# Scores of the first query tile as three products of high and low parts

## What is computed

```python
x = L0_attn_x                                  # (4, 256, 512)
xn = _layernorm(x, axis=-1)
q = _rope((xn @ wq).reshape(B, S, 32, 128), pos)
k = _rope((xn @ wk).reshape(B, S, 8, 128), pos)
v = (xn @ wv).reshape(B, S, 8, 128)
scores = einsum('bqhgd,bshd->bhgqs', q.reshape(B, S, 8, 4, 128), k) * 128 ** -0.5
allowed = (j <= i) & (j > i - 128)             # i query, j key
attn = softmax(where(allowed, scores, finfo.min))
s = einsum('bhgqs,bshd->bqhgd', attn, v).reshape(B, S, 4096) @ wo
g = silu(ffn(xn))                              # 4-bit weights, 1376 hidden
return x + s * g
```

## Time and profile before

| | |
|---|---|
| median of 3 runs | 824.97 us |
| the profiled execution's own time | 827.23 us |
| its span, first to last instruction | 824.8 us |
| TensorE's granted clock over the span | 1.000 of full speed |
| DMA, mean over the span | 54 GB/s |

### The profile page before, as it was taken

The page is one execution under the profiler, slowest core; times in us unless marked ns, Lnnn a source line. Parts: engine busy times, 40 slices in busy tenths (PEclk is TensorE's granted clock), DMA queues, the critical chain, the costliest instruction groups (busy, mean ns, idle before and its releaser), DMA issues.

```text
span 824.8 us, 13612 instructions
## 1 busy us (share of the span) xinstructions
PE 813.2 (99%) x4024; PEld 682.1 (83%) x4024; DVE 556.8 (68%) x1640; ACT 436.3 (53%) x1141; POOL 484.5 (59%) x367
## 2 busy tenths in 40 slices
PE   7999999999999999999999999999999999999997
PEld 4888888888878888888888888888888888888886
DVE  5677757653677667584948576766758494858684
ACT  3432312213866738574666666475747465665762
POOL 1232312326666748674675667486748665677997
PEclk9999999999999999999999999999999999999999
DMA  8434322022011101200020102012001201020112
GB/s 243 131 94 149 109 64 84 29 86 77 15 38 37 41 1 52 77 2 25 25 76 0 51 13 64 0 51 67 9 0 51 76 0 51 0 76 0 52 40 102
DMA packets 43594, 44.55 MB, mean 54 GB/s; under 512 B 3492, under 2 KB 28454, under 8 KB 43558
## 3 DMA queue, kind: packets, MB, share of 16 engines
q1 hardware_dynamic: 43264, 44.05, 18.3%
q10 hardware_dynamic: 296, 0.09, 0.1%
HBM read 42.03 MB, written 2.10 MB: 54 GB/s over the span
## 4 chain that ended last, share of the span: by engine, by line
PE 93%; ACT 2%; DVE 2%; issue 1%; POOL 1%; DMA 1%; SPq 0%; DVEq 0%; POOLq 0%; ACTq 0%
PE bank L1198 26%; PE bank L1199 26%; PE bank L1200 26%; PE bank L1312 3%; PE bank L1334 3%; PE bank L1352 2%; PE bank L1353 2%; PE bank L1354 2%; PE bank L1361 1%; PE bank L1359 1%; PE bank L1358 1%; PE bank L1302 1%; PE bank L1208 1%; DVE probs L993 1%; ACT gate L638 1%
## 5 line engine op out<-in xcount | busy, mean ns | idle before, releaser
L1198 PE MATMUL bank<-xh,wih 128*128 128x512 f32 x384 | 155.2, 404 | 0.3 <-DVE k L950 0.3
L1200 PE MATMUL bank<-xh,wil 128*128 128x512 f32 x384 | 150.0, 391 | 0.0
L1199 PE MATMUL bank<-xl,wih 128*128 128x512 f32 x384 | 150.0, 391 | 0.0
L345 POOL TENSOR_TENSOR swap<-swap,cst 128x512 f32<-128x512 f32 x80 | 106.6, 1333 | 67.7 <-ACT swap L575 67.7
L608 ACT ACTIVATE probs<-probs,nmx 128x128 f32<-128x128 f32 x256 | 99.9, 391 | 71.2 <-DVE nmx L975 70.6
L1198 PE MATMUL bank<-woh,oh 128*128 128x512 f32 x256 | 100.3, 392 | 0.1
L1199 PE MATMUL bank<-wol,oh 128*128 128x512 f32 x256 | 100.0, 390 | 0.0
L1200 PE MATMUL bank<-woh,ol 128*128 128x512 f32 x256 | 99.7, 389 | 0.0
L349 POOL TENSOR_TENSOR q<-q,swap 128x512 f32<-128x512 f32 x64 | 91.3, 1427 | 8.9 <-DVE q L950 5.2
L329 POOL TENSOR_TENSOR wil<-raw,wih 128x512 fp32r<-128x512 f32 x48 | 63.5, 1359 | 42.5 <-ACT wih L557 42.5
L369 POOL TENSOR_TENSOR ph<-ph,cst 128x512 fp32r<-128x512 f32 x32 | 42.0, 1312 | 75.3 <-ACT ph L624 75.3
(11 more groups left out here) (119 smaller groups left out, 1922.0 us busy)
## 6 DMA issues: line engine op xcount, KB each, us to landing
raw<-in_wq SPq DMA_DIRECT2D x32, 256.0 KB, 2.8
raw<-in_wo SPq DMA_DIRECT2D x32, 256.0 KB, 2.9
pk<-in_w SPq DMA_DIRECT2D x44, 128.0 KB, 3.5
sc<-in_s SPq DMA_DIRECT2D x36, 128.0 KB, 3.5
pk<-in_w SPq DMA_DIRECT2D x11, 256.0 KB, 2.5
sc<-in_s SPq DMA_DIRECT2D x11, 256.0 KB, 3.2
xn<-in_x SPq DMA_DIRECT2D x8, 256.0 KB, 5.2
raw<-in_wk SPq DMA_DIRECT2D x8, 256.0 KB, 3.1
```

Source lines behind the costliest of these rows:

```text
L345: nc.gpsimd.tensor_tensor(v, v, spread(sin.unsqueeze(1), P, 2, SEQ), ALU.mult).then_inc(sin_done, 1)
L1198: nc.tensor.matmul(out_, sh, mh, start=(i == 0), stop=False)
L1199: nc.tensor.matmul(out_, sh, ml, start=False, stop=False)
L1200: m = nc.tensor.matmul(out_, sl, mh, start=False, stop=(i == n - 1))
```

## The change

The first query tile gets high and low parts too, `qh0` and `ql0`, in two new SBUF tensors. `kq_hi` and `kq_lo` issue one more instruction for each head. The plain product is replaced by `three` over 128 columns, the keys' parts as they are; `klq_done` is waited for ahead of it, and the wait for `rope_done` on TensorE is gone.

```diff
+        qh0 = sb("qh0", [P, GH, 2, P], f32r, main)
+        ql0 = sb("ql0", [P, GH, 2, P], f32r, main)
...
-        def second(ap):
-
-            return ap.rearrange("p (b t n) -> p b t n", b=2, t=2)[:, :, 1, :]
+        def tiles_of(ap, t):
+
+            return ap.rearrange("p (b t n) -> p b t n", b=2, t=2)[:, :, t, :]
...
-                    nc.scalar.activation(qh[:, c - 1], second(q[:, c - 1]), ACT.Copy).then_inc(khq_done, 1)
+                    nc.scalar.activation(qh0[:, c - 1], tiles_of(q[:, c - 1], 0), ACT.Copy)
+                    nc.scalar.activation(qh[:, c - 1], tiles_of(q[:, c - 1], 1), ACT.Copy).then_inc(khq_done, 1)
...
-                    nc.vector.tensor_tensor(ql[:, c - 1], second(q[:, c - 1]), qh[:, c - 1].bitcast(f32),
+                    nc.vector.tensor_tensor(ql0[:, c - 1], tiles_of(q[:, c - 1], 0), qh0[:, c - 1].bitcast(f32),
+                                            ALU.subtract)
+                    nc.vector.tensor_tensor(ql[:, c - 1], tiles_of(q[:, c - 1], 1), qh[:, c - 1].bitcast(f32),
                                             ALU.subtract).then_inc(klq_done, 1)
...
                 if b == 0:
-                    pe.wait_ge(rope_done, cnt(5, g, bp, h + 2))
+                    pe.wait_ge(klq_done, cnt(5, g, bp, h + 2))
                 wait(pe, masked, cnt(8, g, bp, s - 1))
                 c = b * SEQ
-                nc.tensor.matmul(S_B[s % 2][:, 0:P], q[:, h, c:c + P], k[:, bp, c:c + P], start=True, stop=True)
-                if b == 0:
-                    pe.wait_ge(klq_done, cnt(5, g, bp, h + 2))
+                three(S_B[s % 2][:, 0:P], [(qh0[:, h, b, :], ql0[:, h, b, :], kh[:, bp, c:c + P], kl[:, bp, c:c + P])])
```

## The result

The change makes the kernel slower by 6.1%: 875.52 us (873.55 to 876.58, 4 runs) against 824.97 (824.62 to 825.28), a ratio of 1.061 with a 95% interval of 1.059 to 1.063. Forecast were 873 us, in a range of 850 to 888. The profiled execution took 875.15 us, its span is 873.3, 48.5 more than before's.

What follows compares the result with a forecast made beforehand. TensorE, busy 813.2 of 824.8 us, was taken as the bound. 14.2 + 27.7 + 6 = 48 us on the profiled execution (827.2 to 875), 2.2 less for the median: 873 us, own range 862 to 885, wider range 850 to 888.

Steps and rivals of the forecast that it cites:

- Matrix work: TensorE's scores: three short products paced by their loads, 0.336 against 0.225 us, 128 scores, +14.2 us; bounds -5.0 and +57.6.
- The 81 ns: Skill's pace for each 128-column product in a stream of loads and products: matrix term an estimated +2.3 us, sum 864 us.
- The new operands: Second VectorE subtraction per head loses a turn to GpSimd; TensorE waits, 1.98 us a pair, 14 of 16 pairs, +27.7 us.
- Copies, nothing: ScalarE's extra copy for each of 64 head tiles, 26.5 us in all, was taken to fit in free time at no cost.
- The ends: First and last pair of batches have less beside them to hide in: 3 us each, +6 us.
- hidden loads: Rival on TensorE: loads hide after all, short products take 0.062 us each, 858 us; chance 14%.
- the plain 0.225: Rival on TensorE: each short product takes the plain product's 0.225 us, 905 us; chance 9%.
- the turns were lost: Against the rival that VectorE's extra subtractions cost no turns with GpSimd, leaving only matrix work, 839 us; chance 8%.
- the faster case: Products at 0.062 us and no turn lost to GpSimd, at most 1 us of new waits: 821 us; chance 3%.

Runs made afterwards that it cites:

- products only: Changed kernel without its 64 extra copies and 64 extra subtractions, its short products reading the second query tile's parts: 839.03 us, ratio 1.0176 against the kernel before.
- one wide subtraction: Changed kernel with one copy and one subtraction of 512 columns per head in place of two of 256: 838.58 us, ratio 1.0178 against the kernel before.
- copies only: Kernel before plus ScalarE's 64 extra copies, without the extra subtractions and with the plain product kept: 826.00 us, ratio 1.0026.
- operands only: Kernel before plus the change's extra copies and subtractions, read by nobody, with the plain product kept in the scores: 869.16 us, ratio 1.054.
- near made small: Changed kernel with GpSimd's 64 operations between head 0's two subtractions cut to 4 columns each: 849.92 us, ratio 1.0301 against the kernel before.

## Why the prediction was right

**Matrix work, forecast +14.2.** A score takes 0.69 for 0.575 in the stretch shown, +0.115; over a whole pair with the products only it is +0.107, 13.8 us over 128 scores, and the comparison gives 14.6 (12.6 to 16.4). The choice of 0.112, from the bare load of one idle stretch, was the right one between 0.062 and 0.225; in the trace the starts are 0.113 apart (498.00, 498.12, 498.23), the first of a group excepted. That first one is followed after 0.05, and the first wide product makes up for it (0.17 to the next instead of 0.117), so a single distance misleads and only the whole group is a price. The 81 ns of the Trainium skill ("TensorE: Matmul & The Clock Gate", section "Back-to-back issue gap") do not hold for this type: 0.11 at 128 and at 32 columns. Its section "LDWEIGHTS (loading the stationary operand)" gives columns / 1.2 ns, 107 ns for 128, and the loads that start 0.11 apart agree.

**The new operands, +27.7 for 14 pairs.** A pair took 38.26 us. It takes 41.04 to 41.19 now, in mean 41.10 (254.55 to 790.52 are 13 pairs, one of them with the 1.6 of a stay, below), so 2.84 more; forecast were 2.87. Less the products' 0.86 that leaves 1.98 us for the stands, as forecast, 27.7 over 14. The stand at head 1 was 1.33 for 1.35; that at the output projection is 0.40 and 0.48 in turn for 0.41 (the brackets say 0.25 and 0.32), and each is followed by a bare load of 0.10. That heads 2 and 3 are covered held in all pairs but the last: 15 of the 19 waits for a query's part are head 1's, one where each pair passes to the next, and the other 4 lie before 226 us or behind 798. The two experiments that take a turn away in opposite ways (one wide subtraction, a short operation on GpSimd) show that it is the turns and not VectorE's work, and the one with the operands alone shows that they need no short product beside them.

**Copies, nothing.** In the pairs this holds: with the copies only they are as long as before. The 0.8 to 3.4 us by which that kernel is slower lie elsewhere and are not explained; the forecast had no term for them.

**The ends, +6, and what was not in the sum.** The span grew by 48.5: 13.8 for the products, 27.7 for the pairs, and 7.0 for the rest. In that rest is a stay of TensorE at the lower clock in the pair from 583.42 on, which the forecast did not have; it made that pair 1.6 longer. There is a second stay, from 833.8 to 836.9, and it cost next to nothing, because TensorE has to wait for VectorE behind it. From the output projection to the score that waits there are 8.55 us in the changed kernel, with the stay, and 8.54 with the operands only, which has none there; only the wait differs:

```profile
842.33 0.33 PE L1203 MATMUL bank<-kh,qh 128*128 128x128 f32 x1 [0.64 <-DVE ql L962]
```

```profile
838.71 0.47 PE L1203 MATMUL bank<-kh,qh 128*128 128x256 f32 x1 [1.98 <-DVE ql L962]
```

So about 5.4 are left for the first and the last pair, where the forecast had 6.

**The number.** The sum, 48 for 48.5 on the profiled executions, is better than it could be known: it left out a stay that cost 1.6, and it compares one execution of each kernel. To come from there to the median the forecast took off 2.2, which was how far before's profiled execution lay above its median. The changed kernel's lay 0.4 below its own, so the forecast median is 2.5 too low: 873 for 875.5, a rise of 48 for 50.5.

The rivals fell each by its own sign: the starts are 0.113 apart, which is neither the 0.062 of hidden loads nor the plain 0.225, and the turns were lost (the second subtractions last 1.51 and 1.49); the faster case needed both mild ends.

## What to carry to other kernels

Price a small product by what its operands' loads take and not by its columns: of this type, three of 128 columns cost here as much as three of 256 do (0.113 and 0.117 each). When an instruction that takes turns with another engine's is split or doubled, count the turns, not the work: one subtraction of 512 columns made the kernel 37 us faster here than two of 256 (875.5 to 838.6). And before more work is put on an engine that is not the bound, find who waits for the last of its results, and how much it has in hand: at head 1 it was 1.5 us, and 2.9 were spent.

## What the runs showed of the hardware that had not been expected

TensorE stands for 1.3 and 0.4 or 0.5 us in each pair, and now and then its granted clock falls behind that. The changed kernel at such a place:

```profile
582.15 0.33 PE L1203 MATMUL bank<-kh,qh 128*128 128x128 f32 x1 [1.16 <-DVE ql L962]
...
583.42 0.49 PE L1203 MATMUL bank<-woh,oh 128*128 128x512 f32 x1 [0.32 <-DVE ol L1020]
...
585.37 0.63 PE L1203 MATMUL bank<-woh,oh 128*128 128x512 f32 x1
585.80 0.63 PE L1204 MATMUL bank<-wol,oh 128*128 128x512 f32 x1
```

```profile
582.00:585.00 3.00, 2.53 (x12) 2.01 (x13) 2.92 (x15) 0.88 (x4) 2.53 (x2) 0.89 0.00 0
585.00:588.00 3.00, 3.00 (x9) 2.41 (x8) 1.43 (x7) 1.95 (x10) 0.00 (x0) 0.54 0.00 0
```

The granted clock is 0.54 over the second stretch and 1.00 again from 588 us on. Behind both waits the products start up to 0.43 apart instead of 0.23, from about 584.2 to 587.9, which is the level of 1.2 GHz in place of 2.4, and the pair is 1.6 us longer than its neighbours. The other pairs have the same two waits and no fall, but for the last, where the second stay begins at 833.8 behind waits of 1.76 and 0.24 (by the brackets). With the operands only, where the second wait is 0.6 or 0.7 instead of 0.3, there are five: four behind the two waits of a pair and one behind the single wait of 1.98 at 838.71. The kernel before and all other experiments have none before their end, though with near made small there is a single wait of 1.87 us. So a stand of TensorE can cost more than its length, or, where TensorE waits for another engine behind it anyway, nothing; which stands bring a stay was not tried.
